# Routing to the experts spread over the attention in front and the experts' block, by halves of the batches

## The reference, cut to what matters

```python
x = x + attn_wide(layernorm(x))      # 16 heads of 64
x = x + ffn(layernorm(x))            # experts
x = x + attn_slope(layernorm(x))     # 16 heads of 8, causal, linear bias
x = x + ffn(layernorm(x))            # experts
x = x + attn_rope(layernorm(x)); x = x + group(layernorm(x))
x = x + recurrent(layernorm(x)); x = x + group(layernorm(x))

def ffn(x):                          # 8 experts, cap = 2 * 256 / 8 = 64 tokens each, per batch
    probs = softmax(x @ gate_w)                      # (16, 256, 8)
    top_p, top_idx = top_k(transpose(probs), cap)    # 64 tokens of each (batch, expert)
    xin = take(x, top_idx); h = gelu(xin @ w1); y = (h @ w2) * top_p
    return zeros.at[batch, top_idx].add(y)
```

## Time and profile before

| | us |
|---|---|
| three runs, median | 2280.79 |
| profiled execution, its own time | 2281.49 |
| its span, first to last instruction | 2279.8 |
| PE busy | 2007.5 (88%) |
| VectorE busy | 1556.1 (68%) |
| ScalarE busy | 1174.2 (52%) |
| GpSimd busy | 826.7 (36%) |
| mean granted clock | 0.942 |

### The profile page before, as it was taken

One profiled execution on the slowest core, in us unless ns is written; L12 is line 12 of the kernel. 1 busy time (PEld: TensorE's weight loads), 2 busy tenths in 40 slices (PEclk: granted clock), 3 DMA queues, 4 the chain that ended last, 5 costly groups with the idle time before them and its releaser, 6 DMA issues. The chain is left out here.

```text
span 2279.8 us, 54792 instructions
## 1 busy us (share of the span) xinstructions
PE 2007.5 (88%) x21839; PEld 1331.5 (58%) x21839; DVE 1556.1 (68%) x2782; ACT 1174.2 (52%) x1972; POOL 826.7 (36%) x1276
## 2 busy tenths in 40 slices
PE   5999999999959997999599989997599985479996
PEld 2666666666639995666288966664345542335553
DVE  4787777777764435777554447775688975779984
ACT  3444444444333323666433326665478875447874
POOL 4444444444433432332153414440243323433340
PEclk9999999999979997999799989999699997779998
DMA  5000000000000012443000214440334420124441
GB/s 172 1 1 1 2 1 2 1 1 1 2 6 1 16 45 62 124 120 103 2 4 1 57 30 123 119 121 18 87 103 110 112 62 0 47 79 110 118 115 43
DMA packets 157135, 121.16 MB, mean 53 GB/s; under 512 B 13856, under 2 KB 129456, under 8 KB 156884
## 3 DMA queue, kind: packets, MB, share of 16 engines
q1 hardware_dynamic: 156884, 117.65, 19.1%
HBM read 63.48 MB, written 54.12 MB: 52 GB/s over the span
## 5 line engine op out<-in xcount | busy, mean ns | idle before, releaser
L911 DVE TENSOR_REDUCE l_group_mx<-maxima 128x4 f32<-128x1024 f32 x248 | 304.0, 1226 | 57.0 <-PE maxima L704 55.0
L839 ACT ACTIVATE l_group_pr<-scores 128x1024 f32<-128x1024 f32 x256 | 261.5, 1021 | 71.0 <-PE scores L725 68.5
L2201 POOL TENSOR_TENSOR l_wide_tiles_sum<-l_wide_pr 128x256 f32<-128x256 f32 x256 | 181.0, 729 | 213.6 <-ACT l_wide_pr L2144 213.6
L2172 DVE RECIPROCAL l_wide_rc<-bank 128x256 f32<-128x256 f32 x128 | 224.0, 1750 | 7.2 <-PE bank L2103 5.5
L2144 ACT ACTIVATE l_wide_pr<-scores 128x512 f32<-128x512 f32 x256 | 139.1, 595 | 163.7 <-PE scores L2086 163.7
L2156 DVE TENSOR_REDUCE l_wide_mx<-maxima 128x2 f32<-128x512 f32 x248 | 159.3, 685 | 44.5 <-PE maxima L2066 44.4
L911 DVE TENSOR_REDUCE l_slope_mx<-maxima 128x6 f32<-128x768 f32 x124 | 118.9, 959 | 64.8 <-PE maxima L711 63.2
L2134 ACT ACTIVATE l_wide_qk<-bank 128x512 f32<-128x512 f32 x128 | 76.4, 597 | 157.3 <-PE bank L2050 157.3
L911 DVE TENSOR_REDUCE l_rope_mx<-maxima 128x6 f32<-128x768 f32 x124 | 118.8, 958 | 44.1 <-PE maxima L711 43.1
L839 ACT ACTIVATE l_slope_pr<-scores 128x768 f32<-128x768 f32 x128 | 103.5, 809 | 77.9 <-PE scores L732 77.7
L745 PE MATMUL bank<-l_group_pr,va 128*32 128x256 f32 x2048 | 141.4, 395 | 0.0
(11 more groups left out here) (478 smaller groups left out, 4771.9 us busy)
## 6 DMA issues: line engine op xcount, KB each, us to landing
l_group_st<-stack_dram SPq DMA_DIRECT2D x128, 192.0 KB, 3.8
l_slope_st<-stack_dram SPq DMA_DIRECT2D x64, 192.0 KB, 3.8
l_rope_st<-stack_dram SPq DMA_DIRECT2D x64, 192.0 KB, 3.8
stack_dram<-l_group_parts SPq DMA_DIRECT2D x64, 192.0 KB, 2.3
stack_dram<-l_group_parts SPq DMA_DIRECT2D x64, 128.0 KB, 1.9
stack_dram<-l_slope_parts SPq DMA_DIRECT2D x32, 192.0 KB, 2.4
stack_dram<-l_rope_parts SPq DMA_DIRECT2D x32, 192.0 KB, 2.3
stack_dram<-l_slope_parts SPq DMA_DIRECT2D x32, 128.0 KB, 2.3
```

The lines of the kernel that those rows point to most:

```text
L839: act.activation(pr[:, i % AHEAD, :, 0:keys], Tp[:, :, 0:keys], ACT.Exp).then_inc(s["exps"], 1)
L911: dve.tensor_reduce(mx[:, b % 2, :, :, i], max_bank(i, b)[:, :, 0:BLOCKS * keys].rearrange("p z (a k) -> p z a k", k=keys), AX.X, ALU.max, ...
L2172: own.done(dve.reciprocal(rc[:], Ob[i % 2][:, S:2 * S]))
L2201: pool.tensor_tensor(tiles_sum[:, i % 2, z, :], pr[:, i % 2, z, 0:S], pr[:, i % 2, z, S:2 * S], ALU.add).then_inc(s["added"], 1)
```

## The change

- `route` and its block are gone. A class `Route` does the routing of 8 batches (one half) in pieces: `rstat` (statistics), `rnorm` x8 (two tiles each), `rturn` x4, `rgate` x2, `rback` x2, `rsoft` x2, `rby`, `rtop` x16 (one `max` or one `match_replace`, now on 64 rows), `rplace` x4, `rslot`, and `runit` x5 (norm of the first unit and its split in three).
- Half 0 (batches 0 to 7) runs inside the attention in front (wide, slope), placed slot by slot in `ROUTE_IN_WIDE` and `ROUTE_IN_SLOPE`; statistics and norms are POOL's there, in two `rstat` pieces, with `pow` in place of the square root. `runit` splits the first unit there, on POOL.
- Half 1 (batches 8 to 15) runs in the experts' block by `ROUTE_IN_EXPERTS`, rounds -1 to 2; norms are DVE's, the root is ACT's at the head of the block. The experts' softmax exponential falls in round 1.
- In the experts' block `late` moves from slots 1 and 2 to 3 and 8 of round 0, `pool_setup` behind the split of round 0, and ACT norms and POOL splits only unit 1 at the head.
- Group attention: the masks of a batch come in two halves, each in front of its half of the stack; eight mask DMAs for a batch instead of four, and two waits instead of one.

In the diff the three tables are written short: (round, slot) and the pieces there.

```diff
@@ Route
+    def norm(self, eng, what, i, own):
+        if what == "rstat":
+            self.settled(eng, ROUTED * self.half + 4 * i + 4)
...
+            own.done(eng.tensor_tensor(mean, me, mo, ALU.add))
...
+            if self.normed_on == "pool":
+                own.done(eng.tensor_tensor(rstd, var, self.power[:], ALU.pow))
+            else:
+                eng.sem_inc(s["var"], 1)
+                eng.wait_ge(s["root"], 1)
+                own.done(eng.reciprocal(rstd, rstd))
...
+        else:
+            if i >= 2:
+                self.landed(eng, "rturn", i // 2 - 1)
+            for t in range(NT):
+                ins = eng.tensor_scalar(self.xn[:, i % 2, t, :], K.X[:, tile, :], ..., ALU.mult, ALU.add)
+    def root(self, act):
+        act.wait_ge(self.s["var"], 1)
+        act.activation(self.K.rstd[:, tiles], self.K.var[:, tiles], ACT.Sqrt).then_inc(self.s["root"], 1)
+    def pe(self, pe, what, i, bank):
+        if what == "rturn":
+            pe.wait_ge(s["xn"], 2 * i + 2)
+            for t in range(2 * NT):
+                ins = pe.transpose(...)
...
+        elif what == "rslot":
+            pe.wait_ge(s["slots"], 1)
+    def dve(self, dve, what, i, bank, own):
...
+            if i % 2 == 0:
+                own.done(dve.max(self.top[0:64], self.work[r % 2][0:64]))
+            else:
+                own.done(dve.match_replace(...))
...
+ROUTE_IN_WIDE:  (5,4) rstat.0 (6,1) rnorm.0 (6,2) rnorm.1 (6,3) rturn.0 ... (9,4) rstat.1 ... (11,5) rsoft.1
+    (12,1) rby.0 (12,2) rtop.0 ... (15,2) rtop.15 (15,3)..(15,6) rplace (16,0) rslot.0  (13,1)..(13,5) runit
+ROUTE_IN_SLOPE: (7,5) rstat.0 ... (12,5) rsoft.0 (12,7) rsoft.1 (13,1) rby.0 (13,5) rtop.0 (13,7) rtop.1
+    (14,0) (14,1) (14,5) (14,7) (15,0) (15,1) (15,3)..(15,7) (16,0) (16,1) (16,2) rtop  (16,4) rplace x4 (17,1) rslot.0
+ROUTE_IN_EXPERTS: (-1,3) rstat.0 rnorm.0 rnorm.1 (-1,5) rturn.0 rnorm.2 rnorm.3 (0,0) rturn.1 (0,1) rgate.0
+    (0,2) rnorm.4 rnorm.5 (0,3) rback.0 (0,8) rturn.2 rnorm.6 rnorm.7 (1,0) rturn.3 (1,1) rgate.1
+    (1,3) rback.1 rsoft.0 (1,4) rsoft.1 (1,8) rby.0 (2,0)..(2,7) rtop, two to a slot (2,8) rplace x4 rslot.0
@@ experts
-        route(nc, K, name, W, normed, in_three)
-    late = {1: [("late", 0), ("late", 1)], 2: [("late", 2), ("late", 3)]} if n == 0 else {}
+    late = {3: [("late", 0), ("late", 1)], 8: [("late", 2), ("late", 3)]} if n == 0 else {}
+            normed(act, 1).then_inc(s["xn"], 1)
+            routed.root(act)
             batches(act, tallies, step, UNITS)
-            following.pool_setup(pool)
+                        if n == 0:
+                            following.pool_setup(pool)
+            in_three(pool, own, 1).then_inc(s["in_three"], 1)
@@ narrow_attention, SP
+                if kind == "group" and b >= HOSTED:
+                    sp_masks(sp, b, i)
                 for z in range(2):
                     sp.dma_start(st[...], K.stack_dram[par][...]).then_inc(landed[par][i], 16)
-                if kind == "group" and b >= HOSTED and i == 1:
-                    sp_masks(sp, b)
```

More of the change, by code:

```diff
@@ L235, in norm_stats, with placed @@
     return ((on_vector, finish) if split else on_vector), on_scalar
+E8 = 8
+CAP = 2 * S // E8
+HID = 512
+HC = HID // P
+ROUTED = NB // 2
+ROUTE_BANKED = ("rturn", "rgate", "rback", "rby", "rslot")
+ROUTE_ON = {"rturn": ("pe", "act"), "rgate": ("pe", "act"), "rback": ("pe", "dve"), "rsoft": ("dve", "act"),
+            "rby": ("pe", "dve"), "rtop": ("dve",), "rplace": ("dve",), "rslot": ("pe", "dve"), "rstat": ("norm",), "rnorm": ("norm",), "runit": ("norm",)}
+def placed(table):
+    at = {}
+    for n, slot, pieces in table:
+        for piece in pieces.split():
+            what, i = piece.split(".")
+            at.setdefault((n, slot), []).append((what, int(i)))
+    return at
@@ new lines @@
+ROUTE_IN_EXPERTS = placed([
+    (-1, 3, "rstat.0 rnorm.0 rnorm.1"),
+    (-1, 5, "rturn.0 rnorm.2 rnorm.3"),
+    (0, 0, "rturn.1"),
+    (0, 1, "rgate.0"),
+    (0, 2, "rnorm.4 rnorm.5"),
+    (0, 3, "rback.0"),
+    (0, 8, "rturn.2 rnorm.6 rnorm.7"),
+    (1, 0, "rturn.3"),
+    (1, 1, "rgate.1"),
+    (1, 3, "rback.1 rsoft.0"),
+    (1, 4, "rsoft.1"),
+    (1, 8, "rby.0"),
+    (2, 0, "rtop.0"),
+    (2, 0, "rtop.1"),
+    (2, 1, "rtop.2"),
+    (2, 1, "rtop.3"),
+    (2, 2, "rtop.4"),
+    (2, 2, "rtop.5"),
+    (2, 3, "rtop.6"),
+    (2, 3, "rtop.7"),
+    (2, 4, "rtop.8"),
+    (2, 4, "rtop.9"),
+    (2, 5, "rtop.10"),
+    (2, 5, "rtop.11"),
+    (2, 6, "rtop.12"),
+    (2, 6, "rtop.13"),
+    (2, 7, "rtop.14"),
+    (2, 7, "rtop.15"),
+    (2, 8, "rplace.0 rplace.1 rplace.2 rplace.3 rslot.0"),
+])
@@ L250 @@
 NARROW_BANK = {
-    "slope": {"norm": 1, "qk": 0, "turnmax": 0, "turn1": 1, "v": 0, "turn0": 0},
+    "slope": {"norm": 1, "qk": 0, "turnmax": 0, "turn1": 1, "v": 0, "turn0": 0, "rturn": 1, "rgate": 1, "rback": 1, "rby": 1, "rslot": 1},
     "rope": {"norm": 1, "qk": 0, "swapped": 1, "turnmax": 0, "turn1": 1, "attn": 1, "v": 0, "project": 1, "turn0": 0},
@@ L422, in narrow_walk @@
                     yield what, i, n + a
+            for what, i in routed.get((n, j), []):
+                if engine in ROUTE_ON[what] or (engine == "pool" and "norm" in ROUTE_ON[what]):
+                    yield what, 0, i
 HOSTED = 2
@@ L1504 @@
-EXPERT_BANK = {"gather": (0, 1), "turn": (0, 1, 0, 1), "late": (0, 1, 0, 1)}
+EXPERT_BANK = {"gather": (0, 1), "turn": (0, 1, 0, 1), "late": (0, 1, 0, 1),
+               "rturn": (0, 1, 0, 1), "rgate": (0, 1), "rback": (1, 0), "rby": (0,), "rslot": (1,)}
 def expert_schedule(n, do_a, do_b, do_e):
```

524 lines of the change are left out of this document (348 added, 176 removed).

## The result

Four runs of the changed kernel took 2261.49 to 2265.85 us, median 2264.25, against a median of 2280.59 for the four runs of the kernel before beside them: ratio 0.9927, 95% interval 0.9914 to 0.9939. The forecast was 2250 with a range of 2238 to 2266. The direction held, and the time lies 1.75 us inside the range; the gain was 16 us where 30 were forecast. The profiled execution took 2265.85 (span 2264.1), 15.6 less than the profiled execution before.

What follows compares the result with a forecast made beforehand. PE was taken to bound all three blocks receiving routing work, in slope only just. -63.8 + 17.2 + 0.5 + 4.9 + 5.0 + 6.0 + 1.0 - 1.5 = -30.7 gave 2250 us for the runs, range 2238 to 2266.

Steps and rivals of the forecast that it cites:

- VectorE as the bound: Rival: in slope every round adds its full length, experts' round 2 falls behind, +9 and +5; 2264 us, chance 0.19.
- What goes: Both routing blocks between host attention and experts, 62.2 us, plus PE's 1.66 us wait for GpSimd's one-hots: together -63.8.
- PE's own work: Routing transposes and gates PE must do beside its own work, 4.3 us a half: +17.2, bounds 14 and 20.
- Half 0 in wide: First half's routing inside wide attention fits VectorE's idle time and GpSimd's cover: +0.5, bounds 0 and 5.
- in slope: First half's routing in slope attention: division slots +1.5, `rsoft.0` and copies +1, tail +2.4; sum +4.9, bounds 0 and 14.
- its sign of being wrong: In wide attention, a batch of over 37 us would show the prediction wrong.
- Half 1, the head: Start of the experts' blocks: first `up` delayed to 9.0 to 10.8 us after the iota; +5.0, bounds 2 and 9.
- Half 1, slots: End of experts' round 2: PE stalls about 3.0 us for `rslot`, twice; +6.0, bounds 0 and 9.
- a low clock beyond the first 15 us: In an experts' block, a low clock lasting past its first 15 us would show the prediction wrong.
- The exponential: Experts' round 1: ScalarE's two table loads, 1.28 us each, cause no PE wait; with low clock +1.0, bounds 0 and 5.
- the table rival: Each table switch in experts' round 1 costs a 1.38 us drain, gelu 4 late: +4.4, 2254 us, chance 0.08.
- Masks: Group attention: some 2.6 us of PE's mask waits go, four DMAs issue earlier: -1.5, bounds -2.8 and +1.

Runs made afterwards that it cites:

- twice_turned: Changed kernel with every routing turn doing its four transposes twice into the same place, results the same: 2273.13 us, ratio 0.9967 to the kernel before.
- quiet_pool: Changed kernel with GpSimd starting the split of unit 1 only after the statistics are finished, in both experts' blocks: 2259.93 us, ratio 0.9910 to the kernel before.
- stat_first: Changed kernel with statistics before the first one-hots and their root before unit 1's normalised tiles, in both experts' blocks: 2259.11 us, ratio 0.9905 to the kernel before.
- late_only: Changed kernel with the second half's first two turns, and the work following them, behind the first `up`; split still beside statistics: 2259.99 us, ratio 0.9903.
- early_tops: Changed kernel with the second half's turn to rows, tops and places earlier in rounds 1 and 2, `rslot` unmoved: 2252.40 us, ratio 0.9878 to the kernel before.
- turn_late: Changed kernel with the edits of quiet_pool and late_only together: 2248.28 us, ratio 0.9849 to the kernel before.
- best1: Changed kernel with turn_late and early_tops together, plus the slope attention's last tops and places moved earlier: 2236.75 us, ratio 0.9804 to the kernel before.

## Why the prediction was right and where it failed

The time fell inside the range by luck. The sum said 2250, 14 us off; the range reached 2266 only because it took in a rival, VectorE as the bound at 2264, whose mechanism did not occur: neither in slope (+8.7 in all, 18 by the rival) nor in round 2 did each slot add its length. What failed is the head of the experts' block, then the price of the wait for `rslot`.

**What goes** was right: -62.0 measured for -62.2. No gap over 2.4 us is left between a host and the experts' block, and the wait of 1.66 is gone too. (Of the earlier trace rows, both dips are at five tenths; the prediction read four for the second.)

**PE's own work**, 17.2, was about the right size: 0.44 to 0.67 us for four transposes by twice_turned, 0.56 by the runs, for 0.46.

**Half 0 in wide** and **in slope**: +4.4 for 4.8 and +8.7 for 9.2 in this trace, some 0.8 less by the mean of its like. A wide batch is 37.8 us from residual to residual, not the 35.5 of the window that the prediction took for one; its sign of being wrong, a batch of over 37, was true before the change. After it the longest is 39.5. The tail took 2.59 of slope's part (5.83 before, 8.42 after) for 2.4. The `pow` of 8 columns took 1.67, between the bounds of 1.04 and 2.1, and no wait came of it.

**Half 1, the head**, is the step that failed: `rstat`, "ten small operations of about 0.22", and with it the first `up` "at 9.0 to 10.8". The ten took 6.2, the first `up` came at 13.85, and the head cost +6.8 and +5.8 where +2.8 and +2.2 were forecast. (For rope the sum is off by itself: the long end, 10.8, less 8.08 is 2.7.) Two things stand in its place. VectorE's small operations stop while a GpSimd operation that began before them runs: shown by quiet_pool and stat_first, where the same ten take 1.9. And "these are not last", of the gather copies behind the root, was wrong as soon as the statistics were long: shown by late_only. The earlier trace rows had the warning: eight one-hots of one shape took 5.09 us in one block and 8.61 in the other. I carried that spread into the one-hots only, not into the `rstat` behind them.

The Trainium skill (SBUF — State Buffer, SBUF: two separate sides) has the rule that would have changed this step: VectorE and GpSimd share one pair of ports, whoever starts first holds it for the whole instruction, and the other blocks fully instead of sharing. The ends of the operations in this trace agree, to 0.04 us. The rule names VectorE operations with two SBUF inputs, as L308 and L314 have, or in a two-port mode. The same page (Who interferes with whom) lists copies and operations with a scalar, as L306, L310, L312 and L313 are, among those that can enter such a mode; they were held as long. Which mode they ran in no run here shows.

**Half 1, slots**: the wait for `rslot` was forecast at 3.0 and was 2.70 and 4.53, a mechanism right and its price short. Two things were missing: the hosted work of the rope attention in front of the last places, 1.8 us, and the low clock behind the wait. With both, early_tops takes 10.6 away where the sum had 6.0 for the waits, and 1.0 for table loads and low clock together. The low clock came into this trace and not into quiet_pool's; a low clock beyond the first 15 us was also the prediction's own sign of being wrong, and it came twice, until some 18 us behind the iota and again at the end of round 2.

**The exponential**: no PE wait, as forecast, and the table rival fell. The Trainium skill (ScalarE: Activation LUTs, What ACT_TABLE_LOAD costs) puts a drain of some 1.38 us on each switch; here the load starts 0.01 us behind the activation in front of it, and the next activation 0.01 us after the load of 1.28 has ended, so this measurement decides against it.

**Masks** gave 3.3 for 1.5. The waits that went sum to 2.8, as said; the 1.1 us that I set against them for the four DMAs issued earlier did not show. The last row of the table has -3.8, but its 0.5 beyond that is within the spread of the traces.

Together: head +7.6, `rslot` and its clock +4.6 over the forecast, -0.9 in the hosts and -2.3 behind the second experts' block. The rest of the miss, about 6 us, is in units 0 and 1 behind the head. PE's waits in front of `rback.0`, 0.94 and 0.95, are part of it, and so are about 5 us at the lower clock behind each first `up`. turn_late, whose first `up` has the full clock, gives 1.3 and 1.4 back with the head; how the remainder divides between the low clock and PE's pieces at more than 4.3 a half stays open. Even best1 has +5.0 and +6.2 in rounds -1 to 2.

## What to carry to other kernels

A chain of small VectorE operations must be priced by what GpSimd does beside it; a shape that takes two durations in one trace tells of such a neighbour. Where work is threaded into another block, look for every in-order queue in which it stands in front of the block's own first piece: two such places hide each other, and only both repairs together pay. A wait of PE can cost more than its length: one of 2.7 us cost 1.6 more in the changed kernel's trace and nothing more in quiet_pool's. A price read from one trace should be set beside other traces of the same code; here they differ by 1.6 to 4.3 us in stretches where nothing was changed.

## What the runs showed of the hardware that I had not expected

VectorE operations of 0.17 us (128x16) took 0.9 to 1.0 beside GpSimd operations of 1.0 to 1.5, four norms of 128x128 took 3.94 instead of 1.12, and a scalar operation of 64x256, 0.28 alone in the slope tail, took 1.13 in the experts' block of early_tops. Behind the same PE wait of 2.7 us the granted clock fell to its lower level in six traces of seven, and the next sixteen matmuls took 2.44 to 3.62 us; in the seventh it stayed at the upper level, and they took 1.95.
